# Order of the routed dispatches in a two-layer MoE and attention kernel: second choices behind their own first choices, rewrites by half groups

## Chip, cores and metric

One Trainium2 chip, one of its cores. The metric is the device time of one execution in microseconds; the figure compared is the median of several runs.

## What is computed

8192 tokens of 128 features go through three residual layers: half a feed-forward layer, a linear attention of 16 heads (per batch row of 1024 tokens), half the same feed-forward layer again. The feed-forward layer has a shared part and 16 routed experts, of which each token takes its best two:

```python
logits = xf @ gate_w + gate_b
scores = softmax(logits);  top_vals, top_idx = top_k(scores, 2)
a = silu(xf @ w1[e] + b1[e]) * (xf @ w3[e] + b3[e])         # per chosen expert e
y = sum over the two choices of top_val * (a @ w2[e] + b2[e])
z = silu(xf @ sw1 + sb1) * (xf @ sw3 + sb3) @ sw2 + sb2     # shared part
x = x + 0.5 * (y + z)
```

## The kernel before

The program has five phases, one behind the other, with a barrier of all engines between them: front 0, experts 0, front 1, experts 1, combine. A front normalises the tokens, computes the router's choice and the shared part, and sends every token's row twice into a table in DRAM (xs) that is sorted by expert. An expert phase reads that table in tiles of one expert each and scatters the results to ys. Front 1 also adds experts 0's results and computes the attention. What the change touches lies in the two fronts.

**Tiling.** 64 tiles of 128 tokens; 8 groups of 8 tiles (a group is a batch row), and 16 chunks of 4 tiles, two to a group. A front works in steps s; each engine has its own instruction list, written out by step, and waits on semaphores where it needs another's result. Step s does the routing of group s and, for the group before, six gates m..m+5 (m = 6(s-1)) of the shared part: PE's `ups` into PSUM, ACT's `silus`, DVE's `gates` (line 538), PE's `downs`, then DVE's `outs` (line 548). The shared part's PSUM buffers are few (3 in front 0, 4 in front 1), so a late gate holds ACT and PE up. In front 1, step s also holds the attention of group s+1 (DVE: `phi_q`, `phi_k`, `heads_only`, `attended`), the normalisation of group s+1 for the feed-forward layer (`moments`, `variances`, POOL's power in `scales`, DVE's `shifts`, which writes nm, then ACT's `rows`), and `residual`, `moments_a`, `variances_a`, POOL's `scales_a` and DVE's `shifts_a` of group s+3 and s+2. There is no attention in steps 7 and 8.

**Routing of a group.** DVE: `largest` and `indices` (lines 447 to 472), `hot` (474), `sums` (487), and `places` (493), whose last instruction (line 512) writes the slots, the rows of xs that the tokens go to. In front 0 `places` comes late in step s, in front 1 in its middle.

**Dispatch.** POOL sends one indirect DMA per tile and choice (line 346; 256 in all, 128 a front, 66,560 bytes each): its 128 rows of `xrow` hold 128 features, a destination number (column D) and a weight (column D+1). First and second choice of a token go out of the same row of `xrow`; only the two last columns differ. So the first choice's DMAs must have landed before DVE rewrites these two columns (`rewrite`, lines 514 to 522, two instructions), and the second choice goes out after that. Before the change a rewrite takes a whole group: it waits for the 8 DMAs of the first choice and for a weight from ACT, and then signals `rewrote`.

POOL's order before, in front 0 and front 1 (lines 378 to 389):

```python
for g in range(GROUPS + 1):            # front 0
    first(g)
    second_choice(g - 1)
for s in range(-3, GROUPS + 2):        # front 1
    first(s - 1)
    if 0 <= s + 1 < GROUPS: scales(s + 1)
    if s + 3 < GROUPS: scales_a(s + 3)
    second_choice(s - 2)
```

In front 0 the powers are Newton steps on DVE, and POOL only dispatches. DVE calls `rewrite(s - 2)` in step s, behind the third gate (lines 669 and 730).

**The end of a front.** In step 8 DVE computes the tables of the sorted order (`tables`, lines 616 to 639, after the step's first gate; `tables_out`, 641 to 652, writes `tile_at` last). SP waits for them, then copies 16 blocks of padding rows inside xs (line 299) and waits for their landing. POOL waits for the landing of all second choices (line 390). Then comes the barrier, and the expert phase begins with DVE's memset (line 1257) and SP's loads from xs (line 1233).

Of the kernel before, what the change touches and what calls it, by code (L numbers as in the profile page):

```python
# [18 lines left out]
I32 = mybir.dt.int32  # L19
U32 = mybir.dt.uint32  # L20
ACT = mybir.ActivationFunctionType
ALU = mybir.AluOpType
# [4 lines left out]
D = 128  # L27
# [5 lines left out]
GROUPS = 8  # L33
GT = 8
# [9 lines left out]
CHUNK = 4  # L44
CHUNKS = TILES // CHUNK
# [94 lines left out]
def front(nc, k, sb, ps, n, xa, xs, w=None, ys=None):  # L140

    with phase(nc) as sem, ExitStack() as ctx:
# [4 lines left out]
        xrow = t("xrow", [P, TILES, ROW])  # L147
        dest0 = xrow[:, :, D:D + 1].bitcast(I32).rearrange("p (b i) a -> p b (i a)", i=GT)
        dest1 = t("dest1", [P, TILES], I32)
# [53 lines left out]
        for s_ in range(-3, GROUPS):  # L203
# [18 lines left out]
                 "tab_mm", "tab_done", "pads")  # L222
        (hi, lo, up_h, up, silu, aa, down, outr, chain, tab_in, tab_mm, tab_done, pads) = (
            sem(f"f{n}_{m}") for m in names)
        sent0 = [sem(f"f{n}_sent0{r}") for r in range(3)]

        def of(g):

            return slice(g * GT, (g + 1) * GT)

        with nc.Block(no_gpsimd_drain=True) as block:
# [71 lines left out]
            def _(pool):  # L303
# [37 lines left out]
                          channel_multiplier=2 * GT).then_inc(dests, 1)  # L341
                pool.wait_ge(dests, 1)

                def send(g, q, done):
                    for i in range(g * GT, (g + 1) * GT):
                        pool.indirect_dma_start(  # L346
                            xs, bass.IndirectOffsetOnAxis(slot[:, q, i:i + 1], 0), xrow[:, i, :],
                            None).then_inc(done, 16)

                def scales(g):  # L350
                    pool.wait_ge(var, g + 1)
                    wait(pool, xhr, 2 * (g - 2))
                    pool.tensor_tensor(rs[g % 3][:], ve[g % 2][:], k.nhalf[:], ALU.pow
                                       ).then_inc(rstd, 1)

                def first(g):
                    if not 0 <= g < GROUPS:
                        return
                    pool.wait_ge(slots, g + 1)
                    pool.wait_ge(weighted, g + 1)  # L360
                    pool.wait_ge(xhr, 2 * g + 2)
                    pool.sem_inc(passed, 1)
                    send(g, 0, sent0[g % 3])

                def second_choice(g):
                    if not 0 <= g < GROUPS:
                        return
                    pool.wait_ge(rewrote, g + 1)
                    pool.sem_inc(passed, 1)
                    send(g, 1, sent1)  # L370

                def scales_a(g):
                    pool.wait_ge(var_a, g + 1)
# [2 lines left out]
                                       ).then_inc(rstd_a, 1)  # L376

                if n == 0:
                    for g in range(GROUPS + 1):
                        first(g)  # L380
                        second_choice(g - 1)
                else:
                    for s in range(-3, GROUPS + 2):
                        first(s - 1)
                        if 0 <= s + 1 < GROUPS:
                            scales(s + 1)
                        if s + 3 < GROUPS:
                            scales_a(s + 3)
                        second_choice(s - 2)
                pool.wait_ge(sent1, 16 * TILES)  # L390

            @block.vector
            def _(dve):
# [117 lines left out]
                    dve.wait_ge(atr, g + 1)  # L511
                    dve.tensor_copy(slot[:, :, of(g)], at[:]).then_inc(slots, 1)

                def rewrite(g):
                    dve.wait_ge(sent0[g % 3], 16 * GT * (g // 3 + 1))
                    dve.wait_ge(exp2, g + 1)
                    if g == 0:
                        dve.wait_ge(dests, 1)
                    dve.scalar_tensor_tensor(xrow[:, of(g), D + 1:D + 2], rec[:, of(g)].unsqueeze(2),
                                             0.5, wtop[:, of(g)].unsqueeze(2), ALU.mult, ALU.mult)  # L520
                    dve.tensor_copy(xrow[:, of(g), D:D + 1].bitcast(I32),
                                    dest1[:, of(g)].unsqueeze(2)).then_inc(rewrote, 1)

                def low(c):
                    dve.wait_ge(hi, c + 1)
# [4 lines left out]
                def gates(m):  # L530
                    c, f = divmod(m, 3)
                    if not 0 <= c < CHUNKS:
                        return
                    wd = FEAT[f][1]
                    dve.wait_ge(silu, m + 1)
                    dve.wait_ge(up, m + 1)
                    wait(dve, down, m - 5)
                    dve.scalar_tensor_tensor(  # L538
                        gated[c % 2][0:wd, f], p_hg[(2 * m + 1) % NH][0:wd],
                        k.sb13[0:wd, 1, f:f + 1], sil[m % 2][0:wd], ALU.add, ALU.mult  # L540
                        ).then_inc(aa, 1)
# [112 lines left out]
                def step(s):  # L654
                    m, new, gating = 6 * (s - 1), s + 2 < GROUPS, 0 <= s < GROUPS
                    if 0 <= s < GROUPS - 1:
                        shifts(s + 1)
                    if gating:
                        largest(s)
                        indices(s)  # L660
                    gates(m)
                    if s == GROUPS:
                        tables()
                    gates(m + 1)
                    outs(2 * (s - 1) - 1)
                    if s == GROUPS:
                        tables_out()
                    gates(m + 2)
                    if s >= 2:
                        rewrite(s - 2)  # L670
                    if gating:
                        hot(s)
                    if new:
                        moments(s + 2)
                    gates(m + 3)
                    if gating:
                        sums(s)
                    if new:
                        variances(s + 2)
                        scales(s + 2)  # L680
                    gates(m + 4)
                    outs(2 * (s - 1))
                    if gating:
                        places(s)
                    gates(m + 5)
                    if gating:
                        if n == 0:
                            weight_low(2 * s)
                        low(2 * s)
                        low(2 * s + 1)  # L690
                        if n == 0:
                            weight_low(2 * s + 1)

                def step_1(s):
                    a, b, f, m = s + 1, s + 3, s + 1, 6 * (s - 1)
                    attending, gating = (0 <= g < GROUPS for g in (a, s))
                    if 0 <= s + 2 < GROUPS:
                        shifts_a(s + 2)
                    if attending:
                        phi_q(a, 0)  # L700
                        phi_q(a, 1)
                        phi_k(a, 0)
                        phi_k(a, 1)
                    if gating:
                        largest(s)
                    if attending:
# [20 lines left out]
                        sums(s)  # L727
                        places(s)
                    gates(m + 2)
                    if 0 <= s - 2 < GROUPS:  # L730
                        rewrite(s - 2)
                    if b < GROUPS:
                        residual(b)
                    gates(m + 3)
                    if attending:
                        shifts(f)
                    if s == GROUPS:
                        tables_out()
                    if b < GROUPS:
# [5 lines left out]
                    if gating:  # L745
                        low(2 * s)
                    gates(m + 5)
                    if gating:
                        low(2 * s + 1)

# [688 lines left out]
```

## Time and profile before

| what | us |
|---|---|
| median of 3 runs (lowest to highest) | 983.95 (983.07 to 985.2) |
| the profiled execution | 988.44 |
| its span, first to last instruction | 986.7 |
| PE busy in the span | 792.0 |
| DVE busy | 579.8 |
| POOL busy | 562.8 |
| ACT busy | 470.2 |

All times of the trace are microseconds from the span's start, in the one profiled execution. Front 0 runs from 0 to about 223, experts 0 to about 427, front 1 to about 748, experts 1 to about 950. In a timeline row stand the start, the duration, the engine (SPq is SP's DMA queue), the line of the kernel, the operation, what is written and read, how many instructions the row merges (x), and in brackets how long the engine was idle before and who ended that. POOL's time for a dispatch is the time in which it writes the descriptors, not that of the transfer.

### The profile page before, as it was taken

Reading aid. Unit: us, or ns where it says so; the run is one execution under the profiler, and the core shown is the slowest. Engines: PE = TensorE matmul, PEld = TensorE weight load, DVE = VectorE, ACT = ScalarE, POOL = GpSimd, SP = SyncE. Lnnn points to the kernel's source line nnn. Section 1 sums busy time; section 2 is a strip of 40 time slices with the busy share of each in tenths; the row PEclk is TensorE's granted clock in tenths of the full one; section 3 lists DMA queues with packets and bytes.
Section 4 is the critical chain, followed back from the end, with each engine's and each line's share of the span. In section 5 each row is a group of like instructions: output and inputs, shape, how many; then the busy total and the mean of one; then the engine's idle time right before and its main releaser. Section 6 shows DMA issues by size and latency. Waiting matters only on the chain. (4 is left out here: it accounts for less than half of the span.)

```text
span 986.7 us, 20333 instructions
## 1 busy us (share of the span) xinstructions
PE 792.0 (80%) x5348; PEld 705.0 (71%) x5349; DVE 579.8 (59%) x2112; ACT 470.2 (48%) x967; POOL 562.8 (57%) x584
## 2 busy tenths in 40 slices
PE   2899899847999999806788999899934999999920
PEld 2677777737999999804567777787824999999910
DVE  7688876624555555545557776666722555555536
ACT  3356556313555555415456657665302555555500
POOL 1347777762777777722044266575772777776730
PEclk9799999977999999958779999999976999999965
DMA  9912221132333333241021111010132333333349
GB/s 274 141 45 72 65 68 54 52 92 72 100 105 100 105 101 96 83 164 63 1 65 60 49 44 39 31 48 31 50 97 60 96 101 100 103 102 99 96 166 374
DMA packets 83816, 90.45 MB, mean 92 GB/s; under 512 B 20391, under 2 KB 69421, under 8 KB 82733
## 3 DMA queue, kind: packets, MB, share of 16 engines
q1 hardware_dynamic: 64046, 45.41, 18.3%
q0 software_dynamic: 17408, 35.95, 10.8%
q10 hardware_dynamic: 2304, 8.39, 2.1%
q8 instruction: 27, 0.44, 0.2%
q14 instruction: 31, 0.25, 0.1%
HBM read 47.45 MB, written 44.37 MB: 93 GB/s over the span
## 5 line engine op out<-in xcount | busy, mean ns | idle before, releaser
L1246 POOL DMA_INDIRECT ys<-e_y,e_x x288 | 276.5, 960 | 132.0 <-issue 89.0
L346 POOL DMA_INDIRECT xs<-f_xrow,f_slot x256 | 254.0, 992 | 131.9 <-issue 72.8
L1365 PE MATMUL e_py<-w,e_at 97*128 (+1 forms) x1152 | 152.1, 274 | 0.0
L1365 PEld LDWEIGHTS e_py<-w,e_at 97*128 97x128 f32 (+1 forms) x1152 | 139.9, 191 | 0.1
L1270 DVE TENSOR_TENSOR e_a<-e_pu,e_sil 128x352 f32<-128x352 f32 x144 | 75.6, 525 | 98.2 <-ACT e_sil L1296 96.9
L1277 DVE TENSOR_SCALAR e_y<-e_py,e_x 128x128 f32<-128x128 f32 x288 | 87.8, 347 | 58.9 <-PE e_py L1365 57.9
L1290 ACT ACTIVATE e_xth<-e_px 128x256 fp32r<-128x256 f32 x144 | 55.4, 385 | 131.3 <-PE e_px L1329 130.6
L1296 ACT ACTIVATE e_sil<-e_pu 128x352 f32<-128x352 f32 x144 | 66.9, 464 | 91.0 <-PE e_pu L1342 91.0
L1028 PEld LDWEIGHTS f_pz<-sw,f_gated 128*128 128x128 f32 (+1 forms) x768 | 99.4, 191 | 11.4 <-issue 3.2
L1340 PE MATMUL e_pu<-w13h,e_xth 128*128 x288 | 107.2, 372 | 0.0
L843 ACT ACTIVATE f_sil<-f_phg,sb 128x512 f32<-128x512 f32 (+1 forms) x96 | 65.0, 684 | 84.4 <-PE f_phg L1014 83.7
L1028 PE MATMUL f_pz<-sw,f_gated 128*128 128x128 f32 (+1 forms) x768 | 101.2, 275 | 0.1
L538 DVE SCALAR_TENSOR_TENSOR f_gated<-f_phg,sb,f_sil 128x512 f32<-128x512 f32 (+1 forms) x96 | 71.8, 748 | 49.5 <-ACT f_sil L843 46.2
L1329 PE MATMUL e_px<-ident,e_x 128*128 128x128 f32 x288 | 57.8, 283 | 51.8 <-DMA e_x<-xs 47.5
L1341 PE MATMUL e_pu<-w13l,e_xth 128*128 x288 | 94.2, 327 | 0.0
L1342 PE MATMUL e_pu<-w13h,e_xtl 128*128 x288 | 94.2, 327 | 0.0
L1014 PE MATMUL f_phg<-f_xth,sw13h 128*128 128x512 f32 (+1 forms) x192 | 87.5, 456 | 5.5 <-ACT f_sil L843 5.5
L1302 ACT ACTIVATE e_at<-e_pa 96x512 f32<-96x512 f32 x144 | 85.6, 594 | 2.2 <-PE e_pa L1352 1.6
L1352 PE MATMUL e_pa<-ident,e_a 128*96 128x128 f32 x576 | 86.2, 272 | 0.0
L1014 PE MATMUL f_phg<-f_xtl,sw13h 128*128 128x512 f32 (+1 forms) x192 | 76.7, 399 | 0.0
L1014 PE MATMUL f_phg<-f_xth,sw13l 128*128 128x512 f32 (+1 forms) x192 | 76.4, 398 | 0.0
L1329 PEld LDWEIGHTS e_px<-ident,e_x 128*128 128x128 f32 x288 | 35.9, 145 | 56.3 <-DMA e_x<-xs 50.4
(166 smaller groups left out, 1362.7 us busy)
## 6 DMA issues: line engine op xcount, KB each, us to landing
e_x<-xs SPq DMA_DIRECT2D x288, 65.0 KB
f_yt<-ys SPq DMA_DIRECT2D x16, 512.0 KB, 4.6
c_yt<-ys SPq DMA_DIRECT2D x8, 1024.0 KB, 10.4
ys<-e_y,e_x POOLq DMA_INDIRECT x288
xa<-in_attn_x ACTq DMA_DIRECT2D x8, 512.0 KB, 10.2
xs<-f_xrow,f_slot POOLq DMA_INDIRECT x256, 2.3
out<-xa ACTq DMA_DIRECT2D x8, 512.0 KB
f_raw<-in_ffn_w SPq DMA_DIRECT2D x32, 88.0 KB
```

The source lines that it names most:

```text
L346: pool.indirect_dma_start(xs, bass.IndirectOffsetOnAxis(slot[:, q, i:i + 1], 0), xrow[:, i, :], None).then_inc(done, 16)
L1014: last = pe.matmul(p_hg[(2 * m + g) % NH][0:wd], w_[:, cols], x_[c % NX][:], start=q == 0, stop=q == 2)
L1028: last = pe.matmul(p_z[c % NZ][:, tok], gated[c % 2][0:wd, f, tok], k.sw2[0:wd, f], start=f == 0 and q == 0, stop=f == 2, skip_group_check ...
L1246: pool.indirect_dma_start(ys, bass.IndirectOffsetOnAxis(xin[r][:, t, D:D + 1].bitcast(I32), 0), y[r][:, t, :], None).then_inc(sent[r], 16)
L1277: last = dve.tensor_scalar(y[s][:, t], p_y[j % 2][:, t * D:(t + 1) * D], xin[s][:, t, D + 1:D + 2], None, ALU.mult)
L1302: act.activation(at[r][0:A0], p_a[0:A0], ACT.Copy).then_inc(turned, 1)
L1329: last = pe.transpose(p_x[:, t * P:(t + 1) * P], xin[s][:, t, 0:D], k.ident[:])
L1340: pe.matmul(o, xth[r][:, tok], k.w13h[:, cols], start=True, stop=False)
L1341: pe.matmul(o, xth[r][:, tok], k.w13l[:, cols], start=False, stop=False)
L1342: last = pe.matmul(o, xtl[r][:, tok], k.w13h[:, cols], start=False, stop=True)
L1352: last = pe.transpose(p_a[0:A0, q * P:(q + 1) * P], a[r][:, t, o:o + A0], k.ident[:])
L1365: last = pe.matmul(p_y[r][:, t * D:(t + 1) * D], at[r][0:rows_, q], w2, start=c == 0, stop=c == 1, skip_group_check=True)
```

## The change

Four things change. The completions of first choices are counted per chunk on four semaphores in turn (before: per group on three). A rewrite takes a chunk, half a group: it waits for the 4 DMAs of its own half. POOL sends a group's second choices directly behind its first choices, each half as soon as it is rewritten; in front 1 the power of `scales` stands ahead of the dispatches, and first choices go out in the step in which their slots are written. DVE's order follows: in front 0 the first half's rewrite stands behind the first gate of the next step and the second half's behind the third; in front 1 the first half's stands behind the last gate of the same step, the second half's in the next step behind `phi_q`, ahead of `phi_k`; there `shifts_a` moves behind the two first `phi_k`, and `shifts` ahead of `residual`.

```diff
-        sent0 = [sem(f"f{n}_sent0{r}") for r in range(3)]
+        sent0 = [sem(f"f{n}_sent0{r}") for r in range(4)]
...
-                def send(g, q, done):
-                    for i in range(g * GT, (g + 1) * GT):
+                def send(c, q, done):
+                    for i in range(c * CHUNK, (c + 1) * CHUNK):
...
                     pool.sem_inc(passed, 1)
-                    send(g, 0, sent0[g % 3])
+                    for c in (2 * g, 2 * g + 1):
+                        send(c, 0, sent0[c % 4])
...
-                    pool.wait_ge(rewrote, g + 1)
-                    pool.sem_inc(passed, 1)
-                    send(g, 1, sent1)
+                    for c in (2 * g, 2 * g + 1):
+                        pool.wait_ge(rewrote, c + 1)
+                        pool.sem_inc(passed, 1)
+                        send(c, 1, sent1)
...
                 if n == 0:
-                    for g in range(GROUPS + 1):
+                    for g in range(GROUPS):
                         first(g)
-                        second_choice(g - 1)
+                        second_choice(g)
                 else:
-                    for s in range(-3, GROUPS + 2):
-                        first(s - 1)
+                    for s in range(-3, GROUPS):
                         if 0 <= s + 1 < GROUPS:
                             scales(s + 1)
+                        first(s)
                         if s + 3 < GROUPS:
                             scales_a(s + 3)
-                        second_choice(s - 2)
+                        second_choice(s)
...
-                def rewrite(g):
-                    dve.wait_ge(sent0[g % 3], 16 * GT * (g // 3 + 1))
-                    dve.wait_ge(exp2, g + 1)
-                    if g == 0:
+                def rewrite(c):
+                    if not 0 <= c < CHUNKS:
+                        return
+                    part = slice(c * CHUNK, (c + 1) * CHUNK)
+                    dve.wait_ge(sent0[c % 4], 16 * CHUNK * (c // 4 + 1))
+                    dve.wait_ge(exp2, c // 2 + 1)
+                    if c == 0:
                         dve.wait_ge(dests, 1)
...
@@ step(s), front 0 @@
                     if s == GROUPS:
                         tables()
+                    rewrite(2 * (s - 1))
                     gates(m + 1)
...
                     gates(m + 2)
-                    if s >= 2:
-                        rewrite(s - 2)
+                    rewrite(2 * (s - 1) + 1)
...
@@ step_1(s), front 1 @@
-                    if 0 <= s + 2 < GROUPS:
-                        shifts_a(s + 2)
                     if attending:
                         phi_q(a, 0)
                         phi_q(a, 1)
+                    rewrite(2 * (s - 1) + 1)
+                    if attending:
                         phi_k(a, 0)
                         phi_k(a, 1)
+                    if 0 <= s + 2 < GROUPS:
+                        shifts_a(s + 2)
                     if gating:
                         largest(s)
...
                     gates(m + 2)
-                    if 0 <= s - 2 < GROUPS:
-                        rewrite(s - 2)
+                    if attending:
+                        shifts(f)
                     if b < GROUPS:
                         residual(b)
                     gates(m + 3)
-                    if attending:
-                        shifts(f)
...
                     gates(m + 5)
+                    rewrite(2 * s)
                     if gating:
                         low(2 * s + 1)
```

The two instructions of the rewrite stay as they are, with the slice of a chunk in place of that of a group.

## Rows read from the trace of the kernel before

**Rows 1.** Windows: length; busy PE, PEld, DVE, ACT, POOL; PEclk; DMA share; GB/s.
```profile
208.80:223.40 14.60, 0.00 (x0) 0.00 (x0) 0.63 (x4) 0.00 (x0) 9.01 (x10) 0.61 0.23 69
211.00:212.00 1.00, 0.00 (x0) 0.00 (x0) 0.00 (x0) 0.00 (x0) 0.69 (x2) 1.00 0.40 133
212.00:213.00 1.00, 0.00 (x0) 0.00 (x0) 0.00 (x0) 0.00 (x0) 0.95 (x1) 0.53 0.20 67
724.50:748.30 23.80, 0.00 (x0) 0.00 (x0) 0.29 (x4) 0.00 (x0) 16.03 (x17) 0.56 0.33 82
```

**Rows 2.** Timeline of all engines, last step and end of front 0.
```profile
194.99 0.75 DVE L538 SCALAR_TENSOR_TENSOR f_gated<-f_phg,sb,f_sil 128x512 f32<-128x512 f32 x1 [2.43 <-ACT f_sil L843]
197.50 0.29 DVE L651 CAST tile_at<-f_pg 1x144 int32<-1x144 f32 x1
...
199.25 11.23 SPq L299 DMA_DIRECT2D xs<-xs  x16
...
219.59 0.96 POOL L346 DMA_INDIRECT xs<-f_xrow,f_slot  x1 [0.30 <-issue]
223.40 1.03 DVE L1257 MEMSET e_at<- 1x512 f32 x2 [13.94 <-PEq L73]
```

**Rows 3.** Timeline of all engines, end of front 1.
```profile
719.96 11.12 SPq L299 DMA_DIRECT2D xs<-xs  x16
...
744.44 0.96 POOL L346 DMA_INDIRECT xs<-f_xrow,f_slot  x1 [0.30 <-issue]
748.28 1.03 DVE L1257 MEMSET e_at<- 1x512 f32 x2 [20.31 <-PEq L73]
```

**Rows 4.** Line 346, landings of dispatches started in 30 to 50, then 50 to 190.
```profile
DMA to landing us min/median/max: 4.2/6.0/8.2
...
DMA to landing us min/median/max: 2.3/2.3/3.5
```

**Rows 5.** Timeline of DVE and POOL, group 1 of front 0.
```profile
56.04 0.18 DVE L512 CAST f_slot<-f_at 128x16 int32<-128x16 f32 x1
57.06 1.07 POOL L346 DMA_INDIRECT xs<-f_xrow,f_slot  x1 [15.01 <-DVE f_slot L512]
...
66.11 0.96 POOL L346 DMA_INDIRECT xs<-f_xrow,f_slot  x1 [0.30 <-issue]
```

**Rows 6.** Timeline of DVE, steps 3 and 4 of front 0.
```profile
99.56 0.39 DVE L512 CAST f_slot<-f_at 128x16 int32<-128x16 f32 x1
...
109.54 0.75 DVE L538 SCALAR_TENSOR_TENSOR f_gated<-f_phg,sb,f_sil 128x512 f32<-128x512 f32 x1 [0.34 <-PE f_phg L1014]
...
112.49 0.16 DVE L519 SCALAR_TENSOR_TENSOR f_xrow<-f_rec,f_wtop 128x8 f32<-128x8 f32 x1
```

**Rows 7.** Timeline of DVE, ACT and POOL, steps 4 and 5 of front 1.
```profile
617.27 0.32 DVE L512 CAST f_slot<-f_at 128x16 int32<-128x16 f32 x1
...
621.53 1.65 ACT L811 ACTIVATE f_xrow<-xa,f_nm,f_rs 128x128 f32<-128x128 f32 x4 [2.25 <-DVE f_nm L444]
623.78 0.75 DVE L538 SCALAR_TENSOR_TENSOR f_gated<-f_phg,sb,f_sil 128x512 f32<-128x512 f32 x1 [0.82 <-ACT f_sil L843]
...
625.97 2.02 POOL L375 TENSOR_TENSOR f_rsa<-f_vea,nhalf 128x8 f32<-128x8 f32 x1 [6.66 <-DVE f_vea L578]
...
631.25 0.42 DVE L593 SCALAR_TENSOR_TENSOR f_phk<-f_phk,f_phg 128x256 f32<-128x256 f32 x1
```

**Rows 8.** Timeline of DVE, steps 6 to 8 of front 1.
```profile
681.36 0.18 DVE L512 CAST f_slot<-f_at 128x16 int32<-128x16 f32 x1
...
691.51 0.29 DVE L451 TENSOR_TENSOR f_lgt<-f_pg,gb_s 128x128 f32<-128x128 f32 x1 [0.81 <-PE f_pg L968]
...
700.47 0.18 DVE L512 CAST f_slot<-f_at 128x16 int32<-128x16 f32 x1
...
708.84 0.75 DVE L538 SCALAR_TENSOR_TENSOR f_gated<-f_phg,sb,f_sil 128x512 f32<-128x512 f32 x1 [0.93 <-ACT f_sil L843]
...
716.63 0.75 DVE L538 SCALAR_TENSOR_TENSOR f_gated<-f_phg,sb,f_sil 128x512 f32<-128x512 f32 x1 [2.25 <-ACT f_sil L843]
```

More of the change, by code:

```diff
@@ L512, in places @@
                     dve.tensor_copy(slot[:, :, of(g)], at[:]).then_inc(slots, 1)
-                def rewrite(g):
-                    dve.wait_ge(sent0[g % 3], 16 * GT * (g // 3 + 1))
-                    dve.wait_ge(exp2, g + 1)
-                    if g == 0:
+                def rewrite(c):
[5 more added lines that the diff above has]
+                    if c == 0:
                         dve.wait_ge(dests, 1)
[L519 to L522, printed above, removed]
+                    dve.scalar_tensor_tensor(xrow[:, part, D + 1:D + 2], rec[:, part].unsqueeze(2),
+                                             0.5, wtop[:, part].unsqueeze(2), ALU.mult, ALU.mult)
+                    dve.tensor_copy(xrow[:, part, D:D + 1].bitcast(I32),
+                                    dest1[:, part].unsqueeze(2)).then_inc(rewrote, 1)
                 def low(c):
```

## The prediction

> **What bounds the kernel now.** I looked first at the two places where a routing front hands over to an expert phase. In the last 14.6 us of front 0 (208.80 to 223.40) and the last 23.8 us of front 1 (724.50 to 748.30) PE and ACT do nothing, DVE 0.63 and 0.29 us, and only POOL is busy [rows 1]. The timelines say with what: in front 0 the 128th dispatch starts at 219.59 and the next phase's first DVE instruction at 223.40 [rows 2]; in front 1 they are 744.44 and 748.28 [rows 3]. A landing takes 2.3 us in the median [rows 4], so the dispatches land at 221.9 and 746.7, and barrier and next phase follow 1.5 us later both times. Nothing else in those stretches is as late, except the 16 padding copies that SP issues once DVE has written the tables: issued from 199.25 for 11.23 us, and from 719.96 for 11.12 us [rows 2, 3]. Traffic falls from 133 to 67 GB/s, a dispatch's own, between 211-212 and 212-213 [rows 1], so I put the padding's landing at 212.3, 1.8 after its last issue, and by the same 1.8 at 732.9 in front 1 (estimates). So POOL holds each end back, by 9.6 us in front 0 and 13.8 in front 1; together 23.4. That is what can be won there: the padding copies are late next.
>
> Then I asked why POOL is late. In front 0 group 1's slots are written at 56.22 (56.04 + 0.18), its first dispatch starts 0.84 later at 57.06, its eighth at 66.11 [rows 5]: 9.05 for seven intervals, 1.29 each. Sixteen dispatches take 20.7, with the 0.84 21.5. Slots come every 21.76 (56.04 to 99.56 is two groups [rows 5, 6]). POOL just keeps pace, but second choices run one group late by the program's order, and so one group is left over at the end.
>
> **The change, part by part.** Let S be the end of a group's slots instruction; A and B are its two half groups of four.
>
> *Dispatch order.* No dispatch is added or removed. After S POOL sends A, B (first choices), A, B (second choices): S + 0.84 + 20.7 = S + 21.5, just within the 21.76 period, so it does not fall behind. Group 7's S in front 0 is near 56.22 + 6 x 21.76 = 186.8; its last dispatch is done at 208.3 and landed at 210.6, before the padding's 212.3. In front 1 the last S is 700.65 [rows 8]; 21.5 and 2.3 later is 724.5, far ahead of 732.9. The last two S are only 19.1 apart there (681.54 to 700.65 [rows 8]), so POOL starts the last group 2.4 late: 726.9, still ahead. Both ends pass to the padding: **-9.6 and -13.8**, if compute and tables stay where they are.
>
> They don't quite, because DVE now waits for landings. A has landed at S + 0.84 + 3 x 1.29 + 2.3 = S + 7.0, B at S + 0.84 + 9.05 + 2.3 = S + 12.2; with the longest landing of 50 to 190 us, 3.5 [rows 4], B is S + 13.4. Whatever stands behind the rewrite in DVE's order waits, and PE and ACT behind it through the gates.
>
> *Front 0, rewrite A* stands behind gates(m). There DVE is free at 109.54 - 0.34 = 109.20, S + 9.25 (S = 99.95), and idle for 0.34 [rows 6]: landed long ago, and the two instructions (0.16 each, overlapped, 0.25) fit in the idle time. Cost nothing; without that gap 0.25 a group.
>
> *Front 0, rewrite B* keeps the old place, 112.49 = S + 12.54 [rows 6]. B landed at 12.2: no wait; at 13.4: 0.9. I take the middle, 0.4, for groups 1 to 6 (group 0 has the first gap): **+2.4**, between 0 and 5.4. In the last step A's rewrite stands behind the tables, ahead of a gate that DVE awaits for 2.43 us at 194.99 [rows 2]; it hides there, and tables_out moves by nothing.
>
> *Front 1, powers first, shifts earlier.* ACT's rows wait 2.25 us for DVE's nm, and at the next gate DVE waits 0.82 for ACT [rows 7]. With scales(s+1) ahead of the dispatches and shifts ahead of residual, nm comes earlier by about that wait, and the 0.82 goes; what is late next is DVE's own statistics of the residual. In return rewrite B (0.25) stands ahead of phi_k: net -0.57 in steps with a residual, about -2.8 over five. B has to have landed: phi_k begins at S + 13.66 (631.25 - 617.59 [rows 7]), or 12.84 after the pull, against 12.2. As a late landing takes part of it, I take **-2**, between 0 and -4. Rewrite A comes after the gate that follows the one at 623.78, so after S + 6.9, near its landing at 7.0: nothing. scales_a is now queued behind eight dispatches: done near S + 0.84 + 10.3 + 2.02 [rows 7] = S + 13.2; shifts_a is moved behind two phi_k (0.42 each [rows 7]), past S + 13.9. Nothing; if that cover went, a few tenths a step.
>
> *Front 1, last two groups*, where no attention step lies between. Rewrite B of group 6 comes where DVE stands at 691.51 - 0.81 = 690.70, S + 9.16 [rows 8], and waits till S + 12.2; with 0.25 for itself largest(7) starts at 694.0: **+2.5** (up to 3.7). PE, waiting for the mask, and ACT, for dev, follow. Rewrite B of group 7 stands at the head of the last step, at 708.84 - 0.93 = 707.91, S + 7.26, and holds DVE to S + 12.45 = 713.1: the gate is 4.3 late, and after it tables and padding. Of this up to the 2.25 us that a later gate waits at 716.63 [rows 8] is caught up: **+2.2**, between 2.0 and 5.5.
>
> *Rest.* One more semaphore, 32 short DVE instructions, 16 more waits on POOL: counted above or nothing.
>
> *One page against it.* Dispatches move from a tail with an idle DVE to beside DVE's work. The rows show no price: the one at 66.11, with DVE at work, takes 0.96 like the one at 744.44 [rows 3, 5]. The Trainium skill (SBUF — State Buffer, "SBUF: two separate sides") has it otherwise: while DVE runs a two-port operation, GpSimd is locked out and cannot write descriptors. By it some moved dispatches would grow; by the row the sum needs nothing for it.
>
> **Sum:** -9.6 - 13.8 + 2.4 - 2 + 2.5 + 2.2 = **-18.3 us**. The profiled execution took 988.44 (span 986.7), 4.5 above the median of 983.95; I take the difference from the median: **965.7**.
>
> **Rivals.**
> 1. *Only the padding is left.* Landings of 2.3, and stalls absorbed by gates that wait anyway: -23.4 and about -1 from front 1's steps: 959.5. For it: median landing equals minimum [rows 4]; against: nothing covers the waits of steps 7 and 8.
> 2. *The waits cost their upper ends.* B landing at 3.5: front 0 5.4 instead of 2.4, no gain in front 1's steps, 3.7 and 5.5 at its end: 9.8 more, 975.5. PE could also stand idle long enough for the granted clock to fall, as in the present ends (0.61 and 0.56 [rows 1]).
> 3. *Slower: landings in the middle of a front are late*, since weights or yt are being loaded then. Price: the 6.0 median of the first dispatches [rows 4], 3.7 more at every rewrite B: (12.2 + 3.7 - 12.54) x 6 = 20 in front 0, (15.9 - 12.84) x 6 = 18 in front 1, 7.4 at its end, against the 2.4 counted: +43, 1009. It decides from an extra x where 6(x - 0.34) + 6(x - 0.64) + 2x + 4.7 - 2 = 23.4, x = 1.9: a mean landing of 4.2. For it: 4.2 is the least in 30 to 50 us; against: 50 to 190 us has loads too, and at most 3.5 [rows 4]. The Trainium skill (DMA: Bandwidth & Descriptors, "Queues, rings and completion order") would support it: a semaphore increment lands only after every earlier write of that DMA engine, across its queues; the trace agrees for the first dispatches only.
> 4. *POOL is slowed by DVE.* The program's reason would be the lock-out named above. If each dispatch waited for one gate of 0.75 [rows 6], a group would take 21.5 + 12 = 33.5 against 21.76: seven periods of 11.7 in front 0 alone, +82 - 23, 1043. The 0.96 rows speak against it.
> 5. *No change*: the ends are set by something that follows the dispatches about, the padding copies sharing the DMA engines with them: 983.
>
> **How the numbers follow.** Forecast 0.52, rivals in order 0.18, 0.22, 0.05, 0.01, 0.02. The forecast's own range, by the middle of its terms' bounds, is 961 to 971. The range reaches to rivals 1 and 2: 959 to 976, leaving out about 2 in 10. Faster by over 0.2% (2 us, about what a measurement of this kernel can tell): 0.52 + 0.18 + 0.22 = 0.92; the same 0.02; slower 0.06.
>
> **What would show it.** Right: the last dispatch of each front starts before SP's last padding issue ends; POOL's order in a group is 8 + 4 + 4; the empty ends shrink to about 5 and 9 us of PE idleness; DVE's rewrite waits for "DMA xs" at the head of steps 7 and 8 of front 1 (3 and 5 us) and for under 1 us elsewhere; ACT's 2.25 us wait for nm gone. Wrong: rewrite waits of over 2 us in every step, a period of front 0 well above 21.8, or dispatches still starting after the padding.

## Result and profile after

| | us |
|---|---|
| forecast (range) | 965.7 (959 to 976) |
| before, median of 12 executions | 984.94 (981.48 to 986.63) |
| after, median of 12 executions | 982.75 (970.27 to 987.69) |
| ratio after / before, 95% interval | 0.9938 (0.9909 to 0.9967) |
| profiled execution after (its span) | 985.87 (984.1) |

By this ratio the change wins 0.3 to 0.9%, where 1.9% was forecast. The ratio leaves out the five slowest of the twelve executions after, the profiled one among them, as over 1.5% above the fastest; the medians of all twelve give 0.9978. The executions after the change spread over 17 us, those of the kernel before over 5, so that by all of them the gain is not clear of the spread.

Both ends did what the forecast said. Timeline of the kernel after, both ends (as [rows 2, 3]):

```profile
208.28 11.23 SPq L299 DMA_DIRECT2D xs<-xs  x16
215.45 0.96 POOL L346 DMA_INDIRECT xs<-f_xrow,f_slot  x1 [0.30 <-issue]
223.00 1.02 DVE L1263 MEMSET e_at<- 1x512 f32 x2 [4.90 <-PEq L73]
...
726.63 0.95 POOL L346 DMA_INDIRECT xs<-f_xrow,f_slot  x1 [0.30 <-issue]
...
731.70 11.12 SPq L299 DMA_DIRECT2D xs<-xs  x16
...
746.06 1.02 DVE L1263 MEMSET e_at<- 1x512 f32 x2 [9.69 <-PEq L73]
```

The last dispatch now starts before the last padding copy is issued (208.28 + 11.23 and 731.70 + 11.12), and the next phase follows the padding. But the padding itself begins 9.03 and 11.74 us later than before: what precedes it has become slower. With S for the end of a group's slots instruction, as in the prediction, the fronts divide into three stretches each (us; one profiled execution a kernel, so a column carries the spread of its executions too; the later columns are the experiments below):

| stretch | before | after | late | late0 | tail | f0_only | f1_only | shift | powers_only |
|---|---|---|---|---|---|---|---|---|---|
| front 0, S of group 0 to 7 | 154.87 | 163.70 | 153.78 | 154.47 | 159.84 | 163.44 | 154.16 | 153.31 | 151.84 |
| to the first padding copy | 13.80 | 13.99 | 15.53 | 15.58 | 13.74 | 14.00 | 13.79 | 15.69 | 15.29 |
| to the next phase | 24.15 | 14.72 | 14.97 | 14.70 | 14.71 | 14.68 | 24.69 | 14.73 | 24.10 |
| front 1, S of group 0 to 7 | 209.24 | 215.20 | 205.25 | 212.82 | 205.91 | 209.45 | 214.37 | 214.68 | 202.61 |
| to the first padding copy | 19.31 | 26.23 | 19.23 | 27.32 | 19.33 | 19.13 | 26.65 | 26.69 | 19.50 |
| to the next phase | 28.32 | 14.36 | 14.42 | 14.59 | 14.35 | 27.06 | 14.60 | 14.41 | 34.89 |

The stretches behind the first padding copy lost 9.43 and 13.96 us. The others gained 8.83 + 0.19 + 5.96 + 6.92 = 21.9.

What the others gained is seen in three views. First DVE's waits by what was waited for (total us, times, longest), groups 1 to 6 of front 0 and then all of front 1, kernel after:

```profile
DVE f_xrow L524 <- DMA xs<-f_xrow,f_slot: 5.5, 4, 1.6
...
DVE f_xrow L524 <- DMA xs<-f_xrow,f_slot: 21.4, 11, 3.6
```

L524 is the rewrite's first instruction. Before, it waited once, in step 8 of front 1 (3.2 us). Then single waits, timeline of DVE and, at 697.77, of PE (step 4 of front 0; steps 7 and 8 of front 1):

```profile
116.84 0.17 DVE L524 SCALAR_TENSOR_TENSOR f_xrow<-f_rec,f_wtop 128x4 f32<-128x4 f32 x1 [1.56 <-DMA xs<-f_xrow,f_slot]
...
693.38 0.17 DVE L524 SCALAR_TENSOR_TENSOR f_xrow<-f_rec,f_wtop 128x4 f32<-128x4 f32 x1 [3.57 <-DMA xs<-f_xrow,f_slot]
...
697.77 0.29 PE L984 MATMUL f_pg<-f_mask,tri 128*128 128x128 bf16 x1 [4.82 <-DVE f_mask L486]
...
714.36 0.17 DVE L524 SCALAR_TENSOR_TENSOR f_xrow<-f_rec,f_wtop 128x4 f32<-128x4 f32 x1 [2.23 <-DMA xs<-f_xrow,f_slot]
...
718.83 0.17 DVE L524 SCALAR_TENSOR_TENSOR f_xrow<-f_rec,f_wtop 128x4 f32<-128x4 f32 x1 [3.63 <-DMA xs<-f_xrow,f_slot]
```

DVE waits at 693.38 for group 6's half B; the mask behind it comes late, and PE stands idle for 4.82 us. The windows show what follows such an idleness (columns as in [rows 1]; PEclk is the third from the end), kernel after:

```profile
147.00:150.00 3.00, 0.97 (x9) 0.74 (x9) 2.93 (x10) 1.51 (x3) 0.41 (x1) 0.99 0.07 22
150.00:153.00 3.00, 2.99 (x8) 1.99 (x8) 1.07 (x2) 0.27 (x1) 2.39 (x3) 0.50 0.14 44
...
692.00:696.00 4.00, 0.95 (x9) 0.76 (x7) 2.09 (x22) 0.56 (x3) 2.88 (x4) 1.00 0.16 52
696.00:700.00 4.00, 2.23 (x13) 1.95 (x14) 2.36 (x14) 1.82 (x2) 3.08 (x4) 0.51 0.15 50
```

In the first row of each pair PE is idle for most of the time; in the second the granted clock is 0.50 and 0.51, the lower of its two levels (1.2 GHz) for all or nearly all of the row. In the kernel before, all steps of front 0 from group 1 on show 1.00. PE idles at the head of most of these steps, waiting for DVE, and longer behind a step with a wait; not each such time brings a fall (2.2 us at the head of the step from group 4 brought none). The same place one group later, in the kernel after and in the run late below, whose clock stays at 1.00 there:

```profile
150.01 1.51 PE L1042 MATMUL f_pw<-f_raw,f_centre 128*128 128x352 f32 x2 [2.05 <-DVE w13l L618]
...
143.94 0.53 PE L1043 MATMUL f_pw<-f_raw,f_centre 128*128 128x352 f32 x1 [1.12 <-DVE w13l L618]
```

### The profile page after: what moved, and what is told of

The parts are those of the page before. It is cut to its first block and busy times, and to the rows that moved or that the text cites. A ratio compares the mean times of both kernels' runs of the same rounds, so it can differ in the third digit from the quotient of the medians.

```text
span 984.1 us, 20397 instructions
## 1 busy us (share of the span) xinstructions
PE 805.0 (82%) x5348; PEld 716.1 (73%) x5349; DVE 581.4 (59%) x2144; ACT 469.6 (48%) x967; POOL 560.2 (57%) x584
## 5 line engine op out<-in xcount | busy, mean ns | idle before, releaser
L1034 PEld LDWEIGHTS f_pz<-sw,f_gated 128*128 128x128 f32 (+1 forms) x768 | 102.6, 196 | 16.0 <-DVE f_gated L543 6.4
L1034 PE MATMUL f_pz<-sw,f_gated 128*128 128x128 f32 (+1 forms) x768 | 104.1, 280 | 4.0 <-DVE xa L553 4.0
L1358 PEld LDWEIGHTS e_pa<-ident,e_a 128*96 128x96 f32 x576 | 67.5, 126 | 5.2
```

What stands on the lines that cost most here:

```text
L1034: last = pe.matmul(p_z[c % NZ][:, tok], gated[c % 2][0:wd, f, tok], k.sw2[0:wd, f], start=f == 0 and q == 0, stop=f == 2, skip_group_check ...
L1358: last = pe.transpose(p_a[0:A0, q * P:(q + 1) * P], a[r][:, t, o:o + A0], k.ident[:])
```

## Experiments

Theory 1: the gain of the ends was given back because DVE, which executes in order, waits for landings in front of routing and gates. The rival: the dispatches, moved beside DVE's work, or the moved powers and shifts cost the steps their time, and the waits only show it.

### Take the waits away: late

```diff
 front 0                               front 1
+gates(m + 1); rewrite(A)             +largest(s); rewrite(A)      (step 8: behind tables)
-gates(m); rewrite(A)                 -gates(m + 5); rewrite(A)
+gates(m + 3); rewrite(B)             +hot(s); rewrite(B)          (step 8: behind tables_out)
-gates(m + 2); rewrite(B)             -phi_q; rewrite(B); phi_k
```

> The new order of the dispatches, with every rewrite moved to a place in DVE's list where its half has landed long before (front 0: A behind the second gate, B behind the fourth; front 1: A behind largest, B behind hot, in step 8 behind tables and tables_out). Theory 1 (the 23 us of the two ends were given back because DVE, waiting for landings in its own list, held routing and gates up): the waits for DMA xs go, the steps take what they took before, both ends are set by the padding: 985 - 23.4 = 961.5, between 957 and 967. Rival (the dispatches beside DVE's work, or the moved powers and shifts, cost the steps the time, and the waits only show it): periods of front 0 stay at 23 us or more, time 978 or more.

959.12 us (956.83 to 960.5), ratio 0.9735 (0.9705 to 0.9764). No rewrite waits for a landing any more; windows from S of group 1 to 2 and of group 3 to 4, and both ends, of late:

```profile
55.51:77.31 21.80, 19.80 (x127) 16.41 (x125) 17.36 (x86) 13.03 (x25) 16.41 (x17) 1.00 0.23 67
...
99.17:121.04 21.87, 19.70 (x125) 16.41 (x125) 17.43 (x85) 12.88 (x25) 16.48 (x17) 1.00 0.23 66
```
```profile
199.87 11.23 SPq L299 DMA_DIRECT2D xs<-xs  x16
...
205.99 0.96 POOL L346 DMA_INDIRECT xs<-f_xrow,f_slot  x1 [0.30 <-issue]
214.84 1.02 DVE L1264 MEMSET e_at<- 1x512 f32 x2 [5.16 <-PEq L73]
...
706.03 11.12 SPq L299 DMA_DIRECT2D xs<-xs  x16
...
709.53 0.95 POOL L346 DMA_INDIRECT xs<-f_xrow,f_slot  x1 [0.30 <-issue]
720.45 1.03 DVE L1264 MEMSET e_at<- 1x512 f32 x2 [9.81 <-PEq L73]
```

All dispatches still run beside DVE's work, and the powers are as in the change: the rival is out. Only the place of 64 short instructions differs between 982.75 and 959.12. POOL needs half B rewritten when it has sent A's second choices, at about S + 16 in front 0; the change rewrote it at S + 14 with a wait, late does so at S + 15 without one. The landings did not come sooner: in groups 1 to 6 half B lands at S + 13.1 to 13.9 in late, at S + 12.1 to 14.0 in the change. DVE comes later.

### Which front: f0_only, f1_only, late0, tail

f0_only and f1_only put the other front back to the kernel before; late0 moves the rewrites of front 0 alone; tail moves the three rewrites of groups 6 and 7 in front 1:

```diff
 front 1, steps 7 and 8 (tail)
-(head of step 7) rewrite(6B)         +hot(7); rewrite(6B)
-gates(m + 5); rewrite(7A)            +tables(); rewrite(7A)
-(head of step 8) rewrite(7B)         +tables_out(); rewrite(7B)
```

> The changed kernel with front 1 put back as it was before (its order on POOL and DVE, rewrites by groups). Theory 1: front 0 alone wins 9 us at its end and gives about 9 back in its steps by waits of 1 to 1.5 us for rewrite B and a lower granted clock: 0 to -4 against before, 981 to 985; front 1's steps as before. Rival (front 0 gained as forecast and front 1 lost it all): -7, 978.

> The changed kernel with front 0 put back as it was before. Theory 1: front 1 alone wins 13 us at its end and gives about 12 back by waits of up to 3.6 us and the clock that falls behind them: 0 to -5 against before, 980 to 985. Rival (front 1 gained as forecast and front 0 lost it all): -11, 974.

> The changed kernel with the rewrites moved in front 0 alone (A behind the second gate, B behind the fourth). Theory 1: periods of front 0 back to 21.8, its end 8 us earlier, front 1 as in the changed kernel: 975, between 971 and 978; the moves of both fronts then add up to the 24 us between the changed kernel and the run called late. Rival (front 1's state gives it back): 980.

> The changed kernel with only three rewrites moved, those of the last two groups of front 1: group 6's B behind hot of step 7, group 7's A behind tables and its B behind tables_out of step 8. Theory 1 (their waits of 3.57, 2.23 and 3.63 us hold the last step's routing and the tables up one to one, and a clock fallen behind them adds to it): S6 to S7 of front 1 from 24.8 to about 19.4, S7 to the first padding copy from 26.2 to about 19.3, 12 us less than the changed kernel: 971, between 968 and 974. Rival (tables and padding are late through the steps before, or wait for PE and ACT anyway): 979 or more.

Measured: f0_only 980.72, ratio 0.9961 (0.9936 to 0.9986); f1_only 984.56, 0.9998 (0.9975 to 1.0022); late0 975.44, 0.9883 (0.9857 to 0.9909); tail 974.21 (964.55 to 977.71), 0.9865 (0.9842 to 0.9888). Each front alone gives nearly its whole gain back, as theory 1 says. In ratios, from 0.9938 (after) to 0.9735 (late), front 0's waits hold 0.0055 and the three of the tail 0.0073; the rest, 0.0075, is left to steps 0 to 6 of front 1. These shares hang on the ratio of after: from the 0.9978 of all its executions they are 0.0095, 0.0113 and 0.0035, and the traces are nearer to these (front 0 ends 7.7 us earlier in late0, from S of group 6 to the padding front 1 is 12.1 shorter in tail). tail lies just outside its 968 to 974, though its trace has both steps as forecast; the profiled execution, 964.55, was its fastest. Windows from S of group 6 to S of group 7 and on to the first padding copy, in after and in tail:

```profile
680.65:705.47 24.82, 19.32 (x118) 16.77 (x117) 12.76 (x56) 12.41 (x22) 15.99 (x16) 0.86 0.13 44
705.47:731.70 26.23, 21.49 (x122) 17.41 (x121) 12.85 (x35) 6.12 (x9) 15.32 (x16) 0.87 0.12 41
```
```profile
671.84:691.47 19.63, 17.18 (x119) 14.90 (x118) 12.94 (x56) 12.42 (x22) 14.49 (x15) 1.00 0.15 49
691.47:710.80 19.33, 19.14 (x121) 16.15 (x120) 12.54 (x35) 6.12 (x9) 12.69 (x15) 1.00 0.15 49
```

PE has the same work (x118 to x122) and takes longer for it in after, at a clock of 0.86 and 0.87. f0_only prices the clock, since steps with a wait and steps with a fallen clock follow each other there (S to S, groups 1 to 5):

```profile
56.02:79.14 23.12, 20.18 (x128) 16.45 (x126) 17.58 (x86) 13.89 (x26) 15.42 (x16) 1.00 0.22 65
79.14:104.28 25.14, 23.87 (x123) 20.34 (x124) 17.16 (x86) 11.95 (x23) 15.60 (x16) 0.80 0.20 58
104.28:127.05 22.77, 20.11 (x129) 16.57 (x127) 17.54 (x86) 13.69 (x26) 15.45 (x16) 1.00 0.22 64
127.05:152.20 25.15, 23.88 (x123) 20.34 (x124) 17.25 (x86) 12.15 (x23) 15.60 (x16) 0.80 0.21 58
```

The first and third of these steps contain a wait for half B, of 1.38 and 1.06 us, and take 1.3 and 1.0 more than the 21.8 of late. The second and fourth contain none, but the clock falls at their beginning, and they take 3.3 more. In front 0 such falls came behind steps with a wait alone: before, late and shift have none from group 1 on. They would also explain the spread: of two executions with like waits, S of group 1 to S of group 2 in front 1 took 35.71 at 0.90 (after) and 31.58 at 1.00 (tail). That late too has 34.53 at 0.90 in this one step, without a wait on a landing, stays unexplained.

### Does DVE's place set the wait: early0

```diff
-gates(m + 2); rewrite(B)
+rewrite(B); gates(m + 2)
```

> The changed kernel with front 0's rewrite B one gate earlier, ahead of the third gate in place of behind it: DVE comes to it about 2.3 us sooner, so the wait for the landing grows from 1 to 1.5 us to about 3.5. Theory 1 (a wait on DVE goes one to one into the period of front 0): the steps 1 to 7 grow by about 2 us each, +10 to +15 against the changed kernel's 983. Rival (the gate, PE and ACT take the wait up): within 3 us of the changed kernel.

988.06 us, ratio 1.0037 (1.0012 to 1.0063), 5 more than after: neither forecast. The profiled execution, 985.97, is like that of after, so it does not show those 5. DVE's waits in groups 1 to 6 of front 0 doubled,

```profile
DVE f_xrow L524 <- DMA xs<-f_xrow,f_slot: 12.0, 5, 2.9
```

but the periods hardly grew (23.36 and 23.38 for the waiting steps from groups 2 and 3, against 23.17 in after; all of front 0 from S to S took 162.56 against 163.70). My expectation counted the wait from DVE's arrival. The rewrite begins when half B has landed, at S + 14.05 in after (116.84 - 102.79) and S + 13.63 in early0 (115.30 - 101.67); what sets the period is the landing and the instructions behind it, of which there is one gate more.

### Why half B lands late: shift

The prediction had B landed at S + 12.2, so that DVE, arriving at 12.54, need not wait. Of its last dispatch, one step of after and one of shift (time from dispatch to landing, and who waited):

```profile
L346 POOL DMA_INDIRECT xs<-f_xrow,f_slot x1: 954/954/954, 112.6 to 112.6; - x1
...
  DVE f_xrow L524: 1.6, 1
...
DMA to landing us min/median/max: 4.2/4.2/4.2
```
```profile
L346 POOL DMA_INDIRECT xs<-f_xrow,f_slot x1: 958/958/958, 116.0 to 116.0; - x1
...
DMA to landing us min/median/max: 2.4/2.4/2.4
```

shift differs from after in this alone:

```diff
 PE, ahead of front 0
+for _ in range(128):
+    pe.sem_inc(passed, 1)
```

> The changed kernel with 128 empty semaphore instructions ahead of PE's work in front 0, where PE waits for its first input anyway. In the trace's DMA records a load of 16 KB on the instruction queue falls 11.5 to 15 us behind S in every step of front 0, just while half B's descriptors are written. Theory 1a (it is PE's code, fetched once a step, and it delays half B's landing): the fetch moves by half a step, B lands 2.3 us behind its dispatch, DVE's waits for it in front 0 go under 0.5, the periods to 21.8, the end of front 0 from 223 to about 215; time about 975, with front 1 open. Rival 1b (B lands late for another reason: weights, POOL's queue): waits of 1 to 1.5 and periods of 23 as they were, 983.

The trace's DMA records have one 16 KB transfer a step on the instruction queue, a single record of 0.9 to 1.4 us. Its start after S, and the landing time of B's last dispatch (written from about S + 9.8 on), groups 1 to 6 of front 0:

| group | 1 | 2 | 3 | 4 | 5 | 6 |
|---|---|---|---|---|---|---|
| after: code load at S + | 11.9 | 13.3 | 12.0 | 11.5 | 15.2 | 11.5 |
| after: landing, us | 4.1 | 2.3 | 4.2 | 3.8 | 2.3 | 3.6 |
| shift: code load at S + | 2.2 | 2.9 | 3.0 | 3.0 | 2.3 | 2.3 |
| shift: landing, us | 2.4 | 2.3 | 2.4 | 2.4 | 2.4 | 2.3 |

128 instructions on PE moved the loads, so they are PE's code. With them away the four late landings are gone; DVE's waits in groups 1 to 6 and the landings in that stretch in shift (of its 103 dispatches the profile has landing times for 24, those of half B's first choices):

```profile
DVE f_xrow L524 <- DMA xs<-f_xrow,f_slot: 0.2, 1, 0.2
```
```profile
DMA to landing us min/median/max: 2.3/2.3/2.6
```

Front 0 from S to S took 153.31, less than before. The time, 988.28 (ratio 1.0017, 1.0001 to 1.0033), did not follow: the 128 instructions moved S of group 0 from 30.58 to 37.93, 7.3 us that I had taken for hidden, and front 1 kept its waits (the wait for half A of group 0 alone was 4.37). The mechanism in front 0 is shown; as a cure it is worse than late.

In front 1 no run tests what makes the halves late, but the trace of after points at two more causes. SP loads yt in groups 0 to 2 of this front, and half A of groups 0 and 2 lands beside these loads: the two issued from 557.32 on land 5.4 and 6.2 us later, half A's last two dispatches, from 559.04 on, take 4.5 to 5.0, and DVE waits for them until 564.86. In group 1 POOL's first dispatch takes 3.17 us, beside four TENSOR_TENSOR on DVE (two in the row shown, two right behind it), half B goes out that much later, and DVE waits for it for 2.42 us. Timelines of SP's queue, DVE and POOL, and in the second row the landings of the two dispatches:

```profile
557.32 0.92 SPq L289 DMA_DIRECT2D f_yt<-ys  x2
DMA to landing us min/median/max: 4.5/4.8/5.0
...
519.65 1.28 DVE L561 TENSOR_TENSOR xa<-xa,f_yt 128x512 f32<-128x512 f32 x2
519.88 3.17 POOL L346 DMA_INDIRECT xs<-f_xrow,f_slot  x1 [0.82 <-DVE f_slot L514]
...
534.20 0.17 DVE L524 SCALAR_TENSOR_TENSOR f_xrow<-f_rec,f_wtop 128x4 f32<-128x4 f32 x1 [2.42 <-DMA xs<-f_xrow,f_slot]
```

The Trainium skill (DMA: Bandwidth & Descriptors, "Queues, rings and completion order") says that a semaphore increment lands only behind every earlier write of its DMA engine, across queues; the landings beside the code loads and beside yt agree. The Trainium skill (Runtime: NRT & Kernel Launch, "Instruction fetch mechanics") calls the cost of crossing a 16 KiB boundary of code mostly hidden. No row here prices it for PE; on the landing of another engine's dispatch it was 1.3 to 1.9 us (3.6 to 4.2 against 2.3).

### The change's other parts: group, powers_only, late_powers_behind

```diff
 group (from late): one rewrite of 8 tiles, waiting for both halves
+front 0: gates(m + 2); rewrite(A and B)     +front 1: hot(s); rewrite(A and B)  (step 8: behind tables_out)
 powers_only (from before), POOL; with shifts ahead of residual, shifts_a behind phi_k
+scales(s + 1)
 first(s - 1)
-scales(s + 1)
 late_powers_behind (from late), POOL
-scales(s + 1)
 first(s)
+scales(s + 1)
```

> The kernel of the run called late, with rewrites of whole groups: front 0 behind the third gate, front 1 behind hot, as B there. POOL then has nothing to send between the last descriptor of the first choices and their landing. Theory 1 with halves needed: a group takes POOL 10.3 + 2.3 + 0.6 + 10.3 = 23.5 in front 0 against a period of 21.8, so DVE waits for landings and front 0 gets periods of 23.5 to 24.5, some 10 us more than late; front 1 with its period of 31 stays: 969, between 966 and 974. Rival (the order alone matters, halves add only instructions): 959 to 962.

> The kernel before, with only front 1's moved powers and shifts (scales ahead of the dispatches, shifts ahead of residual, shifts_a behind two phi_k); the dispatch order and the rewrites as before. Theory (the steps gain 4 us, as S0 to S7 of front 1 in the run called late is 205.25 against 209.24, and the first steps before S0 another 1): -4 to -5, 979.5. Rival (those 4 us came from the rewrites' place or from the dispatch order): 984 and S0 to S7 of 209.

> The kernel of the run called late, with front 1's powers (scales) behind the first choices of the same step in place of ahead of them. Theory (the new order needs the powers ahead: a power then waits for 8 dispatches, 10.3 us, and DVE's shifts and ACT's rows for it, some 8 us later than now, in each step from 0 to 6): +40 to +55, about 1005. Rival (rows have slack, as nothing else waited for nm in the changed kernel): within 4 us of 959.

group took 1002.56, ratio 1.0170 (1.0151 to 1.0189). Front 0 is as forecast: periods of 23.0 to 24.2, its end at 225.49, 10.7 behind late. Front 1 I had wrong: 235.63 from S to S instead of 205.25. POOL's timeline there (group):

```profile
628.07 1.03 POOL L346 DMA_INDIRECT xs<-f_xrow,f_slot  x1 [14.40 <-DVE f_xrow L540]
...
637.98 1.67 POOL L353 TENSOR_TENSOR f_rs<-f_ve,nhalf 128x8 f32<-128x8 f32 x1
```

POOL waits 14.40 us for the rewrite behind hot, then sends 8, and only then comes the power on which the next group's rows depend: a loop through POOL of 35 to 39 us a step. The halves let POOL send A meanwhile.

powers_only took 989.19, ratio 1.0030 (1.0016 to 1.0044). From S to S it wins 6.6 us, but the end loses 6.6 (28.32 to 34.89): POOL, one group behind, sends at its own pace,

```profile
711.34 11.12 SPq L299 DMA_DIRECT2D xs<-xs  x16
...
742.38 0.96 POOL L346 DMA_INDIRECT xs<-f_xrow,f_slot  x1 [0.31 <-issue]
746.23 1.03 DVE L1257 MEMSET e_at<- 1x512 f32 x2 [21.32 <-PEq L73]
```

so that neither the theory's -4 nor its rival's unchanged 209 was right: the steps' gain is real and stands unused until the dispatch order changes.

late_powers_behind took 1044.17, ratio 1.0585 (1.0558 to 1.0611), nearly twice the expected loss. DVE's waits in front 1:

```profile
DVE f_nm L446 <- POOL f_rs L353: 82.7, 7, 12.5
```

The stretch from S to S grew by 82.1 against late: each wait for a power behind 8 dispatches went into the step whole. The new order needs the powers ahead.

### What sets the end now: late_pads, late_pads1

```diff
 SP (late_pads: both fronts; late_pads1: front 1 alone)
-for e in range(E): sp.dma_start(xs padding of e)
+for e in range(E // 2): sp.dma_start(xs padding of e)
 ACT, behind its last step
+act.wait_ge(tab_done, 1)
+for e in range(E // 2, E): act.dma_start(xs padding of e)
```

> The kernel of the run called late, with the last 8 of the 16 padding copies issued by ACT's queue in place of SP's. Theory 1 (with the waits gone the padding's 11 us of issue set both ends): the issue takes 5.6 us, the end passes back to the last dispatch, landed 3.3 after its start at 205.99 and 709.53: about 3 us less in front 0 and 5 in front 1, 951. Rival (the ends are set by the dispatches or by the barrier already): 957 to 960.

> The kernel of the run called late, with the second half of the padding copies on ACT's queue in front 1 alone, where ACT is idle by then (in front 0 ACT's last two instructions held its half back to 207.56). Theory: front 0 as in late, front 1's end 4 us earlier: 955, ratio to before about 0.970. Rival (front 1's end is the dispatches'): as late, ratio 0.9735.

late_pads took 958.91, ratio 0.9709 (0.9683 to 0.9736): front 1's last stretch fell from 14.42 to 10.98, front 0's rose from 14.97 to 17.79. There ACT has work of its own left, and its half is issued late (late_pads):

```profile
207.56 5.80 ACTq L973 DMA_DIRECT2D xs<-xs  x8
```

late_pads1 took 953.96 (953.14 to 954.66), ratio 0.9667 (0.9647 to 0.9686), the best kernel here. The end of its front 1:

```profile
703.78 5.68 SPq L300 DMA_DIRECT2D xs<-xs  x8
...
705.77 5.47 ACTq L974 DMA_DIRECT2D xs<-xs  x8
...
707.79 0.96 POOL L347 DMA_INDIRECT xs<-f_xrow,f_slot  x1 [0.30 <-issue]
714.81 1.03 DVE L1274 MEMSET e_at<- 1x512 f32 x2 [5.92 <-PEq L73]
```

So the padding did set the end, as the forecast had it, and halving its issue is worth 3.4 us there (14.42 to 11.03). The ratio fell by twice that from late's; another 3.1 us lie in front 1 from S to S, 202.12 against 205.25, where the two kernels have the same program.

## Why the prediction was wrong, point by point

- **Both ends, -9.6 and -13.8: right.** Measured -9.43 and -13.96, with the padding next, as it said.
- **Dispatch order, POOL's pace: right.** Groups 1 to 7 of front 0 are sent 20.8 to 22.7 us after S (forecast 21.5), and a dispatch keeps its 0.96 in the median. Rival 4 (POOL locked out by DVE) is out at its price: late sends every group beside DVE's work and keeps its periods. Its effect does show in single dispatches, which the rows of the prediction did not: in late's front 0 the first dispatch of each group 1 to 5 starts just behind the first of two TENSOR_TENSOR on DVE and takes 2.0 to 2.1 us in place of 0.96, which alone puts half B 1.0 us later; in front 1 of after it is the 3.17 above. That the one holds the other up is read from their times, not tested.
- **Front 0, rewrite B, +2.4: the step that failed first.** Measured +8.83 from S to S. The 2.3 counted for a landing was right for the first three dispatches of half B (2.3 to 2.7 in all six groups), but the wait goes by the last, and four of its six landings took 3.6 to 4.2, because PE's code load runs beside them. Their mean is 3.4. The prediction had 3.5 as the longest landing and took the middle; but the profile has landing times for only 16 of the 97 dispatches of that stretch, so the row could not bound the others. Rival 3's mechanism, another transfer beside the landing, was the right one: in front 0 the transfer was PE's code and not weights, in front 1 it was yt as well, for half A of groups 0 and 2. The waits of groups 1 to 6 sum to 5.5, as the upper bound's 5.4, and their own steps grew by 3.4; the other 5.5 lie in the two steps that have no wait but a clock of 0.85 and 0.79, named in rival 2 and not priced.
- **Front 1, powers and shifts, -2: mis-sized, then given back.** By themselves they win 6.6, all of it from S of group 0 to S of group 6 (183.52 in powers_only, 190.12 before). The prediction counted ACT's 2.25 for nm and missed why nm was late: in the kernel before the power is issued right behind 8 dispatches (617.63, the last dispatch ending at 617.61). But with the change this stretch took 190.38: rewrites A and B of groups 0 to 3 waited 11.6 us in it, 3.42, 2.42 and 1.99 at the worst places, where the prediction had A at nothing and B at the 0.8 between -2.8 and -2.
- **Front 1, rewrite A, nothing: wrong.** It waited 3.42, 0.87 and 1.49 us for groups 0 to 2 and 2.23 for group 7, at 714.36. Half A landed there at S + 8.9 to 10.1, not at S + 7.0.
- **Step 7, +2.5: mis-sized.** DVE arrived at S + 9.16, as worked out, and waited 3.57 where 3.0 was counted; the step grew by 5.7. Behind the wait PE stood idle for 4.82 us for the mask, and its clock fell to 0.51.
- **Step 8, +2.2: mis-sized.** Two waits in place of one, 2.23 and 3.63; nothing was caught up, and the tables came 6.9 late.
- **Rival 2's sum** is 9.5 by its own terms, not 9.8: 975.2 in place of 975.5. Nothing hangs on it.
- **What would show it.** The order 8 + 4 + 4, the last dispatch ahead of the padding's end and the vanished wait for nm came true. Of the ends, 4.90 and 9.69 us are DVE's idle time; PE's idle time there came to 9.3 and 14.4. Rewrite waits elsewhere stayed neither under 1 us, as named for a right forecast, nor over 2 in every step, as named for a wrong one. The other sign of a wrong one, a period of front 0 well above 21.8 (22.8 to 24.5 from S of group 1 to S of group 6), came true.

Without these waits, in late, the same order of dispatches took 959.12: inside the range, below the 965.7, close to rival 1's 959.5. Rival 1 has the end state right, only the padding left, but not the reason: the landings stayed late, and it was the moved rewrites that kept DVE from waiting for them.

## To carry to other kernels

A wait written into an engine's list is free only if what it waits for has come by then with the slowest landing seen at that place, not the median; place it as late as its consumer allows (here at S + 15 instead of S + 12.5, with POOL needing it at S + 16.3). Price a stall by what it leaves idle: a wait of 1.4 us cost 1.3 in its own step, and 3.3 in the next where PE's clock fell behind it. When a gain at the end does not arrive, divide the phase into stretches and compare each: here the end had been won in full.

## Not expected of the hardware

- A 16 KB load of PE's code, 0.9 to 1.4 us once a step, lengthened the landing of a POOL dispatch from 2.3 us to between 3.6 and 4.2; moved by 128 instructions, it left all 24 known landings of that stretch at 2.3 to 2.6.
- 128 empty semaphore instructions at the head of PE's list delayed the first group by 7.3 us, though PE's first matmul stood at 13.04 us before. The trace has no records of them, so whether all of it is their execution stays open.
- A POOL dispatch that starts beside TENSOR_TENSOR instructions of DVE took 2.1 us (late, front 0) and 3.17 (after, front 1) in place of 0.96.
- The granted clock fell behind two of the three waits of 1.1 to 1.4 us on DVE in f0_only's front 0, to a mean of 0.80 over the next step; that step's loss was over twice the wait's own.
